# A graph attention and mixture-of-experts kernel: the first loads reordered, W1's load and its casts two batches later

## Chip, cores, metric

One core of one Trainium2 chip. The metric is the device time of one launch in microseconds (us), median of the runs shown. Engines: TensorE (PE, its weight loads PEld), VectorE (DVE), ScalarE (ACT), GpSimd (POOL), SyncE (SP), which here only issues transfers.

## What is computed

For 16 graphs of 512 nodes with 128 features (x, float32) and an int32 adjacency (adj, 16 x 512 x 512), one graph attention layer and one mixture of experts, both with a residual. Cut to what matters:

```python
def _L0_gnn_ref(h, adj, W, a):            # h is the layer norm of x
    Wh = jnp.einsum('bni,oi->bno', h, W)
    a1 = a[0, :OUT_F]
    a2 = a[0, OUT_F:]
    si = Wh @ a1
    sj = Wh @ a2
    e = jax.nn.leaky_relu(si[:, :, None] + sj[:, None, :], negative_slope=ALPHA)
    attention = jnp.where(adj > 0, e, NEG_INF)
    attention = jax.nn.softmax(attention, axis=-1)
    h_prime = jnp.einsum('bij,bjo->bio', attention, Wh)
    return jax.nn.elu(h_prime)
...
x = x + _L0_gnn_ref(_layernorm(x, axis=-1), adj, L0_gnn_W, L0_gnn_a)
x = x + _L0_ffn_ref(_layernorm(x, axis=-1), L0_ffn_Wr, L0_ffn_br, L0_ffn_W1, L0_ffn_b1, L0_ffn_W2, L0_ffn_b2, L0_ffn_gamma, L0_ffn_beta)
```

The second layer (`_L0_ffn_ref`) chooses two of eight experts for each graph by the mean of its normed nodes, applies W1, GELU and W2 of both, mixes them and ends with a layer norm.

## The kernel before

Each engine has a program of its own, written out by hand; semaphores tie them together. Nothing is scheduled by a planner: what stands in an engine's program in a row runs in that row.

**Stages.** B = 16 batches (graphs), each of T = 4 tiles of 128 nodes. The attention stage takes the batches one after another, with several in flight: while VectorE computes the logits of batch n (`logits`), it masks and reduces the destination terms of n+1 (`masked_max`), makes the mask of n+2 (`make_mask`) and the norm's statistics of n+4 (`stats1`). This stage takes about the first 145 us. A short router stage follows, then the experts, batch by batch again.

**One batch of attention.** SP loads x(b) (256 KB), GpSimd loads adj(b) (1 MB of int32, cast to 512 KB of bfloat16 on the way, two buffers). TensorE transposes x (`transpose_x`, L1190 in the profile), ScalarE copies it (`copy_xnt`, L951), TensorE projects it with the prepared weights (`project`, L1199), ScalarE scales the rows by the norm's 1/std into whx (`copy_wh`, L964), which GpSimd made from VectorE's statistics (`norms`, L362 and L367). TensorE spreads the destination terms over the partitions by four transposes into one PSUM bank (`spread_dst`, L1210). VectorE turns adj into a mask of 0 and -2^53 (L498), adds it to the spread terms and takes the row maximum (L505). From the maximum come the shifts (L513 to L525), ScalarE computes the leaky part (L972), VectorE the logits (L534), TensorE transposes them (L1233), ScalarE takes the exponential (L1007), TensorE multiplies with whx (L1248).

**Preparing the weights.** gnn_w, a_src and a_dst (semaphore `s_gw`, 48 when all three are in) are loaded once. VectorE centres gnn_w (L480 to L485), TensorE transposes it and multiplies it with both vectors (L1285 to L1287), ScalarE copies the result to `wh_weights` (L1066, semaphore `s_prep`). No batch can be projected before.

**Order of the first loads.** SP: gnn_w, a_src, a_dst, x(0), x(1); then it waits until adj(0) is in, and issues x(2) and x(3). From x(4) on it waits for the mask of batch b-3. Behind x(5) it issues W1 (1 MB, `w1_parts`), behind x(7) the small weights. GpSimd: the identity matrix and three constants, adj(0), the norm of batch 0, adj(1), the norm of batch 1, adj(2) when mask(0) is made, and so on. VectorE: memsets, the centring, `stats1(0)`, `stats1(1)`, `make_mask(0)`, the four `masked_max(0, t)`.

**W1.** ScalarE casts W1's high part in four pieces (`split_w1_hi`, L1028), one at the end of each of its steps 4 to 7. It is read only after the router.

**Fillers.** `keep_busy` (L1181) issues matmuls on an idle tile whose results nobody reads, in TensorE's waits during the first batches.

Of the kernel before, what the change touches and what calls it, by code (L numbers as in the profile page):

```python
# [22 lines left out]
def gat_moe_kernel(nc, x, adj, gnn_w, gnn_a, w_router, b_router, w1, b1, w2, b2, gamma, beta, out):  # L23
    B, N, D = x.shape
    E, _, F = w1.shape
    T = N // P
# [12 lines left out]
    with ExitStack() as ctx:  # L39
# [10 lines left out]
        x_all = sb("x_all", [P, B, T * D])  # L50
# [205 lines left out]
        def _(sp):  # L256
            def load_x(b):
                if b >= 4:
                    sp.wait_ge(s_x[b % 4], 16 * (b // 4))
                sp.dma_start(x_all[:, b, :].rearrange("p (t d) -> p t d", t=T), x_dram[b]).then_inc(s_x[b % 4], 16)  # L260
# [8 lines left out]

            sp.dma_start(gnn_w_sb[:], gnn_w).then_inc(s_gw, 16)  # L270
            sp.dma_start(a_src[:], gnn_a[0:1, 0:D].rearrange("a d -> d a")).then_inc(s_gw, 16)
            sp.dma_start(a_dst[:], gnn_a[0:1, D:2 * D].rearrange("a d -> d a")).then_inc(s_gw, 16)
            load_x(0)
            load_x(1)
            sp.wait_ge(s_adj[0], 16)
            load_x(2)
            load_x(3)
            for b in range(4, B):
                sp.wait_ge(s_mask, b - 3)
                load_x(b)  # L280
                if b == 5:
                    sp.dma_start(w1_parts[:, :, 1, :].bitcast(F32), w1.rearrange("e p f -> p e f")).then_inc(s_w1raw, 16)
                if b == 7:
                    load_small()
# [43 lines left out]
        def _(pool):  # L328
            nc.gpsimd.memset(ident[:], 0.0).then_inc(s_ident, 1)
# [8 lines left out]
            def load_adj(b):  # L338
                if b >= 2:
                    pool.wait_ge(s_mask, b - 1)  # L340
                nc.gpsimd.dma_start(adj_sb[b % 2][:], adj_dram[b]).then_inc(s_adj[b % 2], 16)
# [60 lines left out]
            load_adj(0)  # L402
# [70 lines left out]
        def _(dve):  # L473
# [4 lines left out]

            dve.wait_ge(s_gw, 48)
# [6 lines left out]

            def stats1(b):
                dve.wait_ge(s_x[b % 4], 16 * (b // 4) + 16)
                if b >= 2:
                    dve.wait_ge(s_norm, 2 * (b - 1))  # L490
                for t in range(0, T, 2):
                    nc.vector.bn_stats(bn12[b % 2][:, 0, t:t + 2, :].rearrange("p t k -> p (t k)"),
                                       x_all[:, b, t * D:(t + 2) * D].rearrange("p (t d) -> p d t", t=2)).then_inc(s_bn1, 1)

            def make_mask(b):

                dve.wait_ge(s_adj[b % 2], 16 * (b // 2) + 16)
                nc.vector.tensor_scalar(mask[:], adj_sb[b % 2][:], 0.0, -MASKED, ALU.is_le, ALU.mult).then_inc(s_mask, 1)  # L498
# [113 lines left out]
            stats1(0)  # L612
# [7 lines left out]
            stats1(2)  # L620
            make_mask(1)
            logits(0, 0)
            masked_max(1, 0)
            logits(0, 1)
# [320 lines left out]
        def _(act):  # L945
# [79 lines left out]
            def split_w1_hi(part):  # L1025
                es = slice(part * E // 4, (part + 1) * E // 4)
                act.wait_ge(s_w1raw, 16)
                nc.scalar.copy(w1_parts[:, es, 0, :], w1_parts[:, es, 1, :].bitcast(F32)).then_inc(s_w1hi, 1)  # L1028
# [53 lines left out]
            for n in range(1, B - 1):  # L1082
                step(n)
                if 4 <= n < 8:
                    split_w1_hi(n - 4)
# [88 lines left out]
        def _(pe):  # L1174
# [28 lines left out]
            def spread_dst(b):  # L1203


                pe.wait_ge(s_wh, T * b + T)
                if b >= 1:
                    pe.wait_ge(s_md, T * b)
                for t in range(T):
                    last = nc.tensor.transpose(dst_ps[:, t * P:(t + 1) * P], whx[b % 3][:, t, 0:1].to_broadcast([P, P]),  # L1210
                                               ident[:])
                last.then_inc(s_dst, 1)
# [66 lines left out]
            keep_busy(8)  # L1279
            pe.wait_ge(s_dconst, 2)  # L1280
            pe.wait_ge(s_const, 1)
            transpose_x(0)
            pe.wait_ge(s_gw, 48)
# [6 lines left out]
            keep_busy(5)  # L1290
# [175 lines left out]
```

## Time and profile before

| what | value |
|---|---|
| median of 3 runs | 279.77 us (279.38 to 282.32) |
| the profiled execution's own time | 279.7 us |
| its span, first to last instruction | 277.9 us |
| busy: PE, DVE, ACT, POOL | 91%, 84%, 81%, 55% |
| HBM read, written | 27.48 MB, 4.20 MB |

The profile is one execution; all times in it are microseconds from the span's start. Busy time is work of the engine itself; waiting on a semaphore, and issuing a DMA, does not count. In the order of events a row gives the start, the duration, the engine, the line of the kernel and the tiles, output to the left of the arrow; in brackets at its end the idle time ahead of it and what ended that. A row with "x4" stands for four instructions in succession. A row of SPq or POOL with DMA_DIRECT2D is only the issue; the transfer runs on the 16 DMA engines, q1 for transfers that SP issued, q0 for GpSimd's.

### The profile page before, as it was taken

Reading aid. Unit: us, or ns where it says so; the run is one execution under the profiler, and the core shown is the slowest. Engines: PE = TensorE matmul, PEld = TensorE weight load, DVE = VectorE, ACT = ScalarE, POOL = GpSimd, SP = SyncE. Lnnn points to the kernel's source line nnn. Section 1 sums busy time; section 2 is a strip of 40 time slices with the busy share of each in tenths; the row PEclk is TensorE's granted clock in tenths of the full one; section 3 lists DMA queues with packets and bytes.
Section 4 is the critical chain, followed back from the end, with each engine's and each line's share of the span. In section 5 each row is a group of like instructions: output and inputs, shape, how many; then the busy total and the mean of one; then the engine's idle time right before and its main releaser. Section 6 shows DMA issues by size and latency. Waiting matters only on the chain. (4 is left out here: it accounts for less than half of the span.)

```text
span 277.9 us, 6310 instructions
## 1 busy us (share of the span) xinstructions
PE 252.9 (91%) x1878; PEld 224.0 (81%) x1878; DVE 232.2 (84%) x658; ACT 224.5 (81%) x513; POOL 152.1 (55%) x228
## 2 busy tenths in 40 slices
PE   7888898999889999999988899999999999999950
PEld 3567897888889898889978448999999999999940
DVE  5599999999999999999999873677777777767556
ACT  3377889999999999999999758778888888877820
POOL 4435288777886779887458312343333444444332
PEclk9999999999999999999999979999999999999996
DMA  6999456654366444550000025576545444543112
GB/s 99 211 221 232 93 99 101 113 101 79 69 99 114 85 80 68 78 75 5 0 4 0 0 96 171 201 249 205 180 162 183 156 167 152 172 154 102 50 39 76
DMA packets 40706, 31.57 MB, mean 114 GB/s; under 512 B 2416, under 2 KB 36624, under 8 KB 40672
## 3 DMA queue, kind: packets, MB, share of 16 engines
q1 hardware_dynamic: 31936, 21.72, 24.5%
q0 software_dynamic: 8736, 9.45, 22.5%
q8 instruction: 15, 0.25, 0.3%
q14 instruction: 19, 0.16, 0.2%
HBM read 27.48 MB, written 4.20 MB: 114 GB/s over the span
## 5 line engine op out<-in xcount | busy, mean ns | idle before, releaser
L1248 PE MATMUL banks<-whx,prob_t 128*128 128x129 f32 x512 | 67.9, 277 | 2.8 <-ACT h_att L982 2.6
L1248 PEld LDWEIGHTS banks<-whx,prob_t 128*128 128x128 f32 x512 | 61.8, 192 | 5.5 <-issue 5.5
L384 POOL TENSOR_SCALAR x_all<-x_all,rstd,nb 128x128 f32<-128x128 f32 x56 | 42.4, 769 | 2.9 <-POOL nb L373 2.7
L1127 ACT ACTIVATE logit<-logit,nb,rstd 128x128 f32<-128x128 f32 x60 | 24.8, 483 | 19.7 <-POOL nb L449 19.7
L1233 PE MATMUL banks<-ident,logit 128*128 128x128 f32 x256 | 36.6, 274 | 4.0 <-DVE logit L534 3.2
L1007 ACT ACTIVATE prob_t<-banks 128x512 f32<-128x512 f32 x64 | 38.2, 641 | 1.8 <-PE banks L1233 1.8
L444 POOL TENSOR_SCALAR veps<-mv 128x4 f32<-128x4 f32 x15 | 6.5, 434 | 55.7 <-DVE mv L841 55.7
L367 POOL TENSOR_TENSOR rstd<-var,minus_half 128x8 f32<-128x8 f32 (+1 forms) x20 | 34.2, 1709 | 0.4
L1233 PEld LDWEIGHTS banks<-ident,logit 128*128 128x128 f32 x256 | 29.0, 141 | 6.3 <-DVE logit L534 5.9
L1402 PEld LDWEIGHTS banks<-w2s,masked_even 128*128 128x128 f32 x256 | 29.8, 192 | 0.6
L1402 PE MATMUL banks<-w2s,masked_even 128*128 128x128 f32 x256 | 29.9, 275 | 0.0
L1387 PE MATMUL banks<-x2t_hi,w_pair 128*128 128x512 f32 x64 | 26.8, 418 | 0.0
L825 DVE TENSOR_TENSOR logit<-banks,x_all 128x512 f32<-128x512 f32 x15 | 10.4, 690 | 19.4 <-PE banks L1402 19.4
L1402 PEld LDWEIGHTS banks<-w2s,leaky 128*128 128x128 f32 x224 | 26.1, 192 | 0.5
L1402 PE MATMUL banks<-w2s,leaky 128*128 128x128 f32 x224 | 26.1, 275 | 0.0
L1389 PE MATMUL banks<-x2t_hi,w_pair 128*128 128x512 f32 x64 | 25.1, 391 | 0.0
L1388 PE MATMUL banks<-x2t_lo,w_pair 128*128 128x512 f32 x64 | 25.0, 390 | 0.0
L362 POOL TENSOR_SCALAR var<-bn 128x8 f32<-128x8 f32 (+1 forms) x20 | 5.7, 283 | 32.6 <-DVE bn L561 20.6
L972 ACT ACTIVATE leaky<-masked_even,shift_neg 128x512 f32<-128x512 f32 x32 | 21.2, 721 | 2.8 <-DVE shift_neg L525 2.8
L534 DVE SCALAR_TENSOR_TENSOR logit<-masked_odd,shift_pos,leaky 128x512 f32<-128x512 f32 x32 | 23.2, 747 | 0.3 <-PE banks L1233 0.2
L972 ACT ACTIVATE leaky<-masked_odd,shift_neg 128x512 f32<-128x512 f32 x32 | 21.3, 720 | 2.5 <-DVE shift_neg L525 2.5
L534 DVE SCALAR_TENSOR_TENSOR logit<-masked_even,shift_pos,leaky 128x512 f32<-128x512 f32 x32 | 23.3, 746 | 0.0
(151 smaller groups left out, 574.0 us busy)
## 6 DMA issues: line engine op xcount, KB each, us to landing
adj_sb<-in_adj_dram POOLq DMA_DIRECT2D x16, 512.0 KB, 7.0
w_pair<-w_parts SPq DMA_DIRECT2D x30, 256.0 KB, 2.3
x_all<-in_x_dram SPq DMA_DIRECT2D x16, 256.0 KB, 3.0
w2r<-in_L_ffn_W_dram SPq DMA_DIRECT2D x32, 128.0 KB, 2.1
out_dram<-prob_t SPq DMA_DIRECT2D x15, 256.0 KB, 2.3
w_parts<-in_L_ffn_W_dram SPq DMA_DIRECT2D x1, 1024.0 KB, 8.1
b_mix<-b_spread POOLq DMA_DIRECT2D x1, 704.0 KB, 5.6
out_dram<-prob_t SPq DMA_DIRECT2D x4, 64.0 KB, 1.6
```

Of the source, the lines that this page charges most:

```text
L367: nc.gpsimd.tensor_tensor(rstd[:, kinds, :], var12[:, kinds, :], minus_half[:].unsqueeze(1).to_broadcast([P, 2, T])[:, kinds, :], ALU.pow) ...
L384: nc.gpsimd.tensor_scalar(x_all[:, b, tile], x1_all[:, b, tile], rstd12[c % 4][:, 1, t:t + 1], nb2[c % 2][:, t:t + 1], ALU.mult, ALU.add). ...
L534: nc.vector.scalar_tensor_tensor(out=logit[:, t, :], in0=masked_dst[b % 2][:, t, :], scalar=shift_pos[b % 2][:, t:t + 1], in1=leaky[:, t, ...
L972: nc.scalar.activation(leaky[:, t, :], masked_dst[b % 2][:, t, :], ACT.Identity, bias=shift_neg[:, t:t + 1], scale=ALPHA).then_inc(s_leaky, 1)
L1007: nc.scalar.activation(prob_t[:, t, :], lt_ps[t % 2], ACT.Exp).then_inc(s_prob, 1)
L1127: nc.scalar.activation(zn[par][:, tile], zs[par][:, tile], ACT.Identity, bias=nb3[par][:, t:t + 1], scale=rstd3[par][:, t:t + 1]).then_inc ...
L1233: last = nc.tensor.transpose(lt_ps[t % 2][:, c * P:(c + 1) * P], logit[:, t, c * P:(c + 1) * P], ident[:])
L1248: last = nc.tensor.matmul(into[:, 0:D + 1], prob_t[:, t, c * P:(c + 1) * P], whx[b % 3][:, c, 2:WHX], start=(c == 0), stop=(c == T - 1))
L1387: nc.tensor.matmul(hid_ps[kc], lo, x2t_hi[par][:], start=True, stop=False)
L1388: nc.tensor.matmul(hid_ps[kc], hi, x2t_lo[par][:], start=False, stop=False)
L1389: nc.tensor.matmul(hid_ps[kc], hi, x2t_hi[par][:], start=False, stop=True).then_inc(s_hid_ps, 1)
L1402: last = nc.tensor.matmul(y_ps[par][:, t * D:(t + 1) * D], hidden[par][:, kc, t * P:(t + 1) * P], w2s[par][:, kc // FC, kc % FC, :], start ...
```

## The change

Seven edits, all in the order of things:
- GpSimd issues adj(0) as its first instruction, ahead of the identity matrix.
- SP issues x(0) ahead of gnn_w, a_src and a_dst.
- x(2) waits for the prepared weights (`s_prep`), no longer for adj(0); x(3) still waits for adj(0).
- W1's load stands behind x(7) instead of x(5), the small weights behind x(9) instead of x(7); ScalarE's four casts of W1 follow steps 6 to 9 instead of 4 to 7.
- VectorE computes the statistics of x(0) ahead of centring the weights; `logits(0, 0)` comes ahead of `make_mask(1)` and `logits(0, 1)` ahead of `masked_max(1, 0)`.
- For batch 0, `spread_dst` waits tile by tile for whx instead of for all four tiles.
- Fewer fillers at the start: 4 instead of 8, a new one behind `transpose_x(0)`, 3 instead of 5 behind `project(0)`.

```diff
+            load_x(0)
             sp.dma_start(gnn_w_sb[:], gnn_w).then_inc(s_gw, 16)
             sp.dma_start(a_src[:], gnn_a[0:1, 0:D].rearrange("a d -> d a")).then_inc(s_gw, 16)
             sp.dma_start(a_dst[:], gnn_a[0:1, D:2 * D].rearrange("a d -> d a")).then_inc(s_gw, 16)
-            load_x(0)
             load_x(1)
+            sp.wait_ge(s_prep, 1)
+            load_x(2)
             sp.wait_ge(s_adj[0], 16)
-            load_x(2)
             load_x(3)
             for b in range(4, B):
                 sp.wait_ge(s_mask, b - 3)
                 load_x(b)
-                if b == 5:
+                if b == 7:
                     sp.dma_start(w1_parts[:, :, 1, :].bitcast(F32), w1.rearrange("e p f -> p e f")).then_inc(s_w1raw, 16)
-                if b == 7:
+                if b == 9:
                     load_small()
...
         def _(pool):
+            nc.gpsimd.dma_start(adj_sb[0][:], adj_dram[0]).then_inc(s_adj[0], 16)
             nc.gpsimd.memset(ident[:], 0.0).then_inc(s_ident, 1)
...
-            load_adj(0)
             norms(0)
             load_adj(1)
...
+            stats1(0)
             dve.wait_ge(s_gw, 48)
             nc.vector.bn_stats(w_stats[:], gnn_w_sb[:]).then_inc(s_centre, 1)
...
-            stats1(0)
             stats1(1)
             make_mask(0)
...
             stats1(2)
+            logits(0, 0)
             make_mask(1)
-            logits(0, 0)
+            logits(0, 1)
             masked_max(1, 0)
-            logits(0, 1)
             masked_max(1, 1)
...
-                if 4 <= n < 8:
-                    split_w1_hi(n - 4)
+                if 6 <= n < 10:
+                    split_w1_hi(n - 6)
...
-                pe.wait_ge(s_wh, T * b + T)
-                if b >= 1:
+                if b >= 1:
+                    pe.wait_ge(s_wh, T * b + T)
                     pe.wait_ge(s_md, T * b)
                 for t in range(T):
+                    if b == 0:
+                        pe.wait_ge(s_wh, t + 1)
...
-            keep_busy(8)
+            keep_busy(4)
             pe.wait_ge(s_dconst, 2)
             pe.wait_ge(s_const, 1)
             transpose_x(0)
+            keep_busy(1)
             pe.wait_ge(s_gw, 48)
...
             project(0)
-            keep_busy(5)
+            keep_busy(3)
             spread_dst(0)
```

SP's row from the program's start, before. The names are the tile written and the tensor read; a mark in brackets names the semaphores waited for, `adj_loaded0` is `s_adj[0]`.

```order
L270 DMA gnn_w_sb<-in_L0_gnn_W_dram 128x128
L271 DMA a_src<-in_L0_gnn_a_dram 128x1
L272 DMA a_dst<-in_L0_gnn_a_dram 128x1
L260 DMA x_all<-in_x_dram 128x4x128 x2
L260 DMA x_all<-in_x_dram 128x4x128 [waits adj_loaded0]
L260 DMA x_all<-in_x_dram 128x4x128
L260 DMA x_all<-in_x_dram 128x4x128 [waits x_loaded0,mask_ready]
L260 DMA x_all<-in_x_dram 128x4x128 [waits x_loaded1,mask_ready]
L282 DMA w1_parts<-in_L0_ffn_W1_dram 128x8x256
```

The same place in the changed program:

```order
L260 DMA x_all<-in_x_dram 128x4x128
L271 DMA gnn_w_sb<-in_L0_gnn_W_dram 128x128
L272 DMA a_src<-in_L0_gnn_a_dram 128x1
L273 DMA a_dst<-in_L0_gnn_a_dram 128x1
L260 DMA x_all<-in_x_dram 128x4x128
L260 DMA x_all<-in_x_dram 128x4x128 [waits gnn_weights_ready]
L260 DMA x_all<-in_x_dram 128x4x128 [waits adj_loaded0]
L260 DMA x_all<-in_x_dram 128x4x128 [waits x_loaded0,mask_ready]
L260 DMA x_all<-in_x_dram 128x4x128 [waits x_loaded1,mask_ready]
L260 DMA x_all<-in_x_dram 128x4x128 [waits x_loaded2,mask_ready]
L260 DMA x_all<-in_x_dram 128x4x128 [waits x_loaded3,mask_ready]
L283 DMA w1_parts<-in_L0_ffn_W1_dram 128x8x256
```

x(0) has moved from the fourth place to the first, x(1) stays the fifth, x(2) has another wait, and W1 stands behind two more loads of x.

VectorE's row from its last memset to the first masked maximum, before (bn12_0 and bn12_1 hold the statistics of batch 0 and 1):

```order
L477 MEMSET whx2 128x524
L480 BN_STATS w_stats<-gnn_w_sb 128x6 [waits gnn_weights_loaded]
L481 TENSOR_SCALAR a_src_scaled<-a_src 128x1
L483 BN_AGGR w_mean<-w_stats 128x2 [waits gnn_weights_centred]
L485 TENSOR_SCALAR gnn_w_centred<-gnn_w_sb,w_mean 128x128 [waits gnn_weights_centred]
L492 BN_STATS bn12_0<-x_all 128x6 [waits x_loaded0]
L492 BN_STATS bn12_0<-x_all 128x6
L492 BN_STATS bn12_1<-x_all 128x6 [waits x_loaded1]
L492 BN_STATS bn12_1<-x_all 128x6
L498 TENSOR_SCALAR mask<-adj_sb0 128x2048 [waits adj_loaded0]
L505 ISA masked_even,dst_max<-mask,banks 128x512 [waits dst_in_psum,mask_ready]
```

The same place in the changed program:

```order
L478 MEMSET whx2 128x524
L485 BN_STATS bn12_0<-x_all 128x6 [waits x_loaded0]
L485 BN_STATS bn12_0<-x_all 128x6
L490 BN_STATS w_stats<-gnn_w_sb 128x6 [waits gnn_weights_loaded]
L491 TENSOR_SCALAR a_src_scaled<-a_src 128x1
L493 BN_AGGR w_mean<-w_stats 128x2 [waits gnn_weights_centred]
L495 TENSOR_SCALAR gnn_w_centred<-gnn_w_sb,w_mean 128x128 [waits gnn_weights_centred]
L485 BN_STATS bn12_1<-x_all 128x6 [waits x_loaded1]
L485 BN_STATS bn12_1<-x_all 128x6
L500 TENSOR_SCALAR mask<-adj_sb0 128x2048 [waits adj_loaded0]
L507 ISA masked_even,dst_max<-mask,banks 128x512 [waits dst_in_psum,mask_ready]
```

The statistics of x(0) have changed places with the centring of the weights; the statistics of x(1), the mask and the maximum keep theirs.

## Rows read from the trace of the kernel before

**Rows 1.** The page's first part: busy us, share of the span, instructions.

```profile
span 277.9 us, 6310 instructions
## 1 busy us (share of the span) xinstructions
PE 252.9 (91%) x1878; PEld 224.0 (81%) x1878; DVE 232.2 (84%) x658; ACT 224.5 (81%) x513; POOL 152.1 (55%) x228
```

**Rows 2.** Busy us (instructions) in stretches; behind them PEclk, DMA share, GB/s.

```profile
12.00:20.00 8.00, 7.29 (x52) 5.10 (x51) 7.90 (x24) 5.63 (x14) 4.21 (x5) 1.00 1.08 227
47.88:56.58 8.70, 8.27 (x71) 7.63 (x70) 8.70 (x26) 8.18 (x21) 6.95 (x10) 1.00 0.53 91
74.02:82.88 8.86, 8.14 (x70) 7.62 (x70) 8.71 (x26) 8.73 (x22) 7.11 (x10) 1.00 0.52 89
```

In a row of this view the five busy times are, in this order, those of PE, PEld, DVE, ACT and POOL.

**Rows 3.** Order of events from 0 to 16 us: start, duration, engine, line, tiles.

```profile
0.74 0.20 POOL L329 MEMSET ident<- 128x128 f32 x1 [0.29 <-POOLq L1454]
0.75 0.39 SPq L270 DMA_DIRECT2D gnn_w_sb<-in_L_gnn_W_dram  x1
...
1.46 3.59 PE L1181 MATMUL banks<-idle_in 128*128 128x512 bf16 x8 [1.46 <-DVE idle_in L474]
...
1.66 0.43 SPq L272 DMA_DIRECT2D a_dst<-in_L_gnn_a_dram  x1
...
1.94 0.99 POOL L341 DMA_DIRECT2D adj_sb<-in_adj_dram  x1 [0.30 <-POOL expert_iota L334]
...
3.73 0.29 DVE L480 BATCH_NORM_STATS2 w_stats<-gnn_w_sb 128x6 f32<-128x128 f32 x1 [0.52 <-DMA a_dst<-in_L_gnn_a_dram]
...
4.28 0.29 DVE L485 TENSOR_SCALAR gnn_w_centred<-gnn_w_sb,w_mean 128x128 f32<-128x128 f32 x1
4.87 0.76 DVE L492 BATCH_NORM_STATS2 bn<-x_all 128x6 f32<-128x256 f32 x2 [0.30 <-DMA x_all<-in_x_dram]
...
5.86 0.42 PE L1285 MATMUL banks<-ident,gnn_w_centred 128*128 128x128 f32 x1
...
6.68 0.27 ACT L1066 COPY wh_weights<-banks 128x130 f32<-128x130 f32 x1
...
7.00 1.16 PE L1199 MATMUL banks<-wh_weights,xnt 128*128 128x130 f32 x8 [0.36 <-ACT wh_weights L1066]
7.03 0.83 POOL L341 DMA_DIRECT2D adj_sb<-in_adj_dram  x1
...
8.00 1.24 PE L1181 MATMUL banks<-idle_in 128*128 128x512 bf16 x5
8.20 1.15 ACT L964 ACTIVATE whx<-banks,rstd 128x130 f32<-128x130 f32 x4 [1.25 <-PE banks L1199]
...
9.40 0.65 PE L1210 MATMUL banks<-ident,whx 128*128 128x128 f32 x4 [0.16 <-ACT whx L964]
10.22 0.77 DVE L492 BATCH_NORM_STATS2 bn<-x_all 128x6 f32<-128x256 f32 x2 [4.59 <-DMA x_all<-in_x_dram]
...
11.61 0.69 DVE L505 CUSTOM_DVE_ANT_0 masked_even<-mask,banks 128x512 f32<-128x512 bf16 x1
```

**Rows 4.** Order of events on SP alone, from 1.5 to 6 us.

```profile
2.13 0.98 SPq L260 DMA_DIRECT2D x_all<-in_x_dram  x2
```

**Rows 5.** Waits from 0 to 34 us: us in total, times, longest; SP's from 0 to 80.

```profile
SPq L260 <- DMA adj_sb<-in_adj_dram: 6.9, 1, 6.9
...
DVE bn L492 <- POOL rstd L367: 0.6, 1, 0.6
```

**Rows 6.** DMA queues: packets, MB, share of 16 engines; two rows 5-6 us, one 8-9.

```profile
q0 software_dynamic: 140, 0.14, 93.8%
q1 hardware_dynamic: 11, 0.01, 2.8%
...
q1 hardware_dynamic: 242, 0.12, 45.3%
```

**Rows 7.** Order of events from 16 to 34 us: W1's load, and the mask of batch 3.

```profile
16.44 0.50 SPq L282 DMA_DIRECT2D w_parts<-in_L_ffn_W_dram  x1
...
30.60 0.68 DVE L498 TENSOR_SCALAR mask<-adj_sb 128x2048 bf16<-128x2048 bf16 x1
```

More of the change, by code:

```diff
@@ L477, in _, with stats1 @@
                 nc.vector.memset(whx[i][:], 1.0).then_inc(s_dconst, 1)
+            def stats1(b):
+                dve.wait_ge(s_x[b % 4], 16 * (b // 4) + 16)
+                if b >= 2:
+                    dve.wait_ge(s_norm, 2 * (b - 1))
+                for t in range(0, T, 2):
+                    nc.vector.bn_stats(bn12[b % 2][:, 0, t:t + 2, :].rearrange("p t k -> p (t k)"),
+                                       x_all[:, b, t * D:(t + 2) * D].rearrange("p (t d) -> p d t", t=2)).then_inc(s_bn1, 1)
+            stats1(0)
             dve.wait_ge(s_gw, 48)
@@ L485, in _ @@
             nc.vector.tensor_scalar(gnn_w_centred[:], gnn_w_sb[:], w_mean[:, 0:1], None, ALU.subtract).then_inc(s_centre, 1)
[L487 to L493, printed above, removed]
             def make_mask(b):
```

## The prediction

> **What bounds the kernel now.** I read the busy shares first, then the stretches, then the order of events of the first 16 us, then the DMA queues. VectorE's share is 84% of 277.9 us [rows 1], an average over stages, so it is read by stage. The table of stretches [rows 2] takes whole batches of the attention stage, one from each mask to the next: VectorE is busy 8.70 of 8.70 us and 8.71 of 8.86. VectorE sets the pace there, and a batch takes about 8.7 us; from the mask at 30.60 [rows 7] to the one at 47.88, where the second stretch begins, it is 17.3 us for two. A chain of batches that runs on one full engine has a simple property: whatever moves its first batch moves everything after it by the same amount. So the first 12 us are worth reading.
>
> There VectorE is nearly idle. Its own rows [rows 3]: the statistics of x(0) at 4.87, then nothing for 4.59 us until x(1) has landed (10.22), the mask, the first masked maximum (11.61). Between x(1) landing and that maximum lie 11.61 - 10.22 = 1.39 us of VectorE work. From 11.61 on the engine hardly stops: 7.90 of the 8 us from 12 to 20 [rows 2]. The maximum needs two inputs: the mask, which needs adj(0) and stands behind the statistics of x(1) in VectorE's queue; and the spread destination terms in PSUM, which TensorE finished at 9.40 + 0.65 = 10.05 [rows 3]. So the load side ends last, by 11.61 - 10.05 = 1.56 us. Both loads of it are late together: SP issued x(0) and x(1) from 2.13 to 3.11 [rows 4] and then waited 6.9 us for adj(0) [rows 5], until 10.0; VectorE's wait for x(1) ended at 10.22. GpSimd had issued adj(0) at 1.94, so it took 8.1 us. x(0) was there by 4.87, 2.7 us after its issue; x(1), issued near 2.6, took about 7.6 us. The queues say why [rows 6]: from 5 to 6 us adj(0)'s queue q0 moved 140 packets and held 93.8% of the engines' time, while q1, with x(1) in it, moved 11; from 8 to 9 us q1 moved 242.
>
> **The change part by part.**
>
> adj(0) first. The DMA leaves GpSimd's queue behind the constants (1.94) for the place of the first memset (0.74): 1.2 us earlier. The identity's memset and select and the two constants behind them, which all lay between 0.74 and 1.94, now end one issue of 0.99 us later, by 2.9 at the latest, ahead of x(0)'s landing; that cover hides them. adj(0) then lands at 10.0 - 1.2 = 8.8.
> GpSimd's issue now lies beside VectorE's first memsets. It did before too: it took 0.99 us there, against 0.83 for the next [rows 3]. By the Trainium skill (SBUF — State Buffer, the box on how DVE blocks software-generated DMA) GpSimd can't write descriptors while VectorE holds the shared port; by that the gain could shrink by the remaining memset, but these rows show at most 0.16 us, which I leave out.
>
> x(0) first. From 2.13 to 0.75, 1.4 us earlier; it lands at about 0.75 + 2.7 = 3.5. VectorE is free from 3.73 - 0.52 = 3.2 on [rows 3], its statistics run 3.5 to 4.25, and what lay between their start (4.87) and the issue of adj(1) (7.03), 2.2 us of statistics and GpSimd's norm, puts that issue at 5.7.
>
> The weights behind it. gnn_w, a_src and a_dst are issued some 0.46 us later each; a_dst at 2.13 in place of 1.66 [rows 3]. Before, VectorE's wait for it ended at 3.73, 2.07 us after its issue. With x(0)'s 256 KB ahead in the same queue I put it at 4.7: the lower bound is 2.13 + 2.07 = 4.2, the upper is that it fares like x(1), which took 7.6 us, so 9.7. I am near the lower bound because adj(0)'s queue starts slowly: x(0), which was under way when q0 began, still took only 2.7 us. From a_dst to the spread terms: VectorE 4.57 - 3.73 = 0.84; TensorE and ScalarE 5.86 to 6.95 = 1.1 for the weights' transposes and copy; the projection 1.16; ScalarE's four copies 1.15, by 0.04 apart; and, since the wait is now by tile, only the last transpose, 0.2 to 0.3. Sum 4.6, with gaps 4.9. So the terms are ready at 4.7 + 4.9 = 9.6, before the mask. TensorE has fewer fillers (4 for 8, 1 new, 3 for 5). The first eight take 3.59 us, 449 ns each, five later ones 1.24 us, 248 ns each [rows 3]: the lower and the higher of its two clock levels (1.2 and 2.4 GHz), although the granted clock prints 1.00. If its gaps delay the rise, this chain has the projections at the lower level and grows by some 1 us; 9.6 becomes 10.6, still near the mask. That costs little.
>
> x(1) itself. Its place in SP's row is the old one, the fifth DMA, issued near 2.6 as before. What gets earlier is the traffic it stands against: adj(0) begins and ends 1.2 us sooner. But adj(1) too comes 1.3 us sooner, and in x(1)'s own queue as many bytes stand ahead. Bounds for its landing: 10.2 - 1.4 = 8.8 if everything slides with x(0), and 10.2 if nothing does; below nothing, 10.2 + 1 if the weights' 256 tiny packets now share turns with q0. I take 9.4, since the later of both loads is held up by adj(0) more than by its own issue. Then the first masked maximum starts at 9.4 + 1.4 = 10.8 in place of 11.61: -0.8 us. The spread terms (9.6) and adj(0) (8.8) are earlier than that.
>
> x(2) is released by the prepared weights (near 7.5) instead of adj(0); its use is the third statistics at about 13.8, no gain, no loss. Logits(0,0) before mask(1) and logits(0,1) before the maximum: the same instructions on a full VectorE, 0. They give TensorE and ScalarE work some 0.6 us earlier, which would matter only if VectorE waited for them. Its one gap there is 0.6 us for GpSimd's rstd [rows 5], which stands behind the statistics of x(3), in the same place as before: 0. Range of this pair: -0.3 to +0.2.
>
> W1's load two batches later (1 MB, issued at 16.44 before [rows 7], near 31 after) clears the stretch 16 to 24 us, where VectorE's only wait is that for rstd [rows 5], and goes beside adj(5), which is issued at about the same time and whose mask is the one at 47.88. Before, the load beside W1 was adj(3), and its mask at 30.60 had no wait [rows 7]. So 0. The four casts of W1 on ScalarE move from steps 4 to 7 to steps 6 to 9. The stretch from 74.02, which holds one, has ScalarE at 8.73 us in place of 8.18 and takes 8.86 us in place of 8.70 [rows 2], so four casts cost at most 0.6 us; moved, I expect the same: 0, with ±0.3.
>
> Sum: -0.8 us. The profiled execution of before took 279.7 us with its span of 277.9, the median of the runs is 279.77, so both bases agree. 279.8 - 0.8 = 279.0 us.
>
> **The rivals.**
>
> A, nothing arrives earlier. x(1) is issued when it was and its queue holds the same bytes; if its landing at 10.2 is its own, VectorE starts as before. For: the same position in SP's row. Against: q1 moves 11 packets in a microsecond while adj(0) has the engines [rows 6], so its landing is not its own. Result 279.7, ±0.3.
>
> B, slower: the weights behind adj(0). q1 nearly stands still when q0 has come into flow, 11 packets against 140 [rows 6]. Before, that met x(1), which had room. Now gnn_w, a_src and a_dst are in it, 384 packets if each of their 3 x 128 rows is one, and the chain of 4.9 us hangs on them. It decides from the point where a_dst lands later than 11.6 - 4.9 = 6.7. At the middle rate between 11 and 242 packets per us, some 100, from 4.4 on they land at 8.2: VectorE's first maximum comes at 13.1, +1.5 us, result 281.3. For: the starved microsecond lies 1.2 us earlier, at 4 to 5 us, where they are. Against: x(0) itself, with q0 beginning, was not held up.
> The Trainium skill (DMA: Bandwidth & Descriptors, "Queues, rings and completion order") says each engine takes turns between queue rows by whole packets of some 9 to 17 descriptors; by that each of the three small loads could wait for a turn of adj(0)'s, which speaks for B. The rows here neither show the turn's length nor deny it.
>
> C, the full slide. x(1) lands at 8.8, a_dst at 4.2, the maximum starts at 10.2 (-1.4), and the earlier logits close part of a gap in the first batches (-0.3): 278.1.
>
> **How the numbers follow.** My forecast (about -0.8) 0.42, A 0.25, C 0.21, B 0.12. The range: down to C with its last gap and the casts' gain (-0.3), 277.7; up to most of B, 280.9. One percent of 279.8 is 2.8 us, about what a measurement of this kernel can tell from no change. Faster than 277.0 would need 1.1 us more than C: 0.04. Slower than 282.6 would need the weights to land at 9.5: 0.03. Within 1%: 0.93.
>
> **What would show it.** In the profile after: GpSimd's adj(0) issue at about 0.75; VectorE's first statistics at 3.5 with x(0) as releaser; centred weights at about 5.1 to 5.6; x(1)'s statistics at 9.4; the first maximum at 10.8; the mask that was at 47.88 at about 47.1, and the first W1 cast two batches (17.4 us) later, less the shift. It is wrong if the first maximum waits for the spread terms (B), if x(1)'s statistics stay at 10.2 (A), or if a shift seen at 11 us is gone by 31 us, which would say that VectorE's queue had slack there.

## The result, and the profile after

The changed kernel takes 285.54 us (median of 4 runs, 282.87 to 287.09) against 279.57 for the kernel before on the same chip: a ratio of 1.0176, 95% interval 1.0114 to 1.0238. Run again later beside the experiments it took 283.98 us (6 runs, 282.89 to 286.77), ratio 1.0121, interval 1.0063 to 1.018. It is slower, and by more than the range allowed. The medians and ranges of this document are over all executions; the ratios leave out four executions that are over 1.5% above their kernel's fastest (two of e2's, one each of e3's and e4's, see below), and are not quotients of the medians.

The order of events of the changed kernel, from 0 to 16 us, as [rows 3] of before:

```profile
0.75 0.45 SPq L260 DMA_DIRECT2D x_all<-in_x_dram  x1
...
1.27 0.99 POOL L330 DMA_DIRECT2D adj_sb<-in_adj_dram  x1 [0.82 <-POOLq L1458]
...
2.27 0.43 SPq L273 DMA_DIRECT2D a_dst<-in_L_gnn_a_dram  x1
...
3.61 0.76 DVE L485 BATCH_NORM_STATS2 bn<-x_all 128x6 f32<-128x256 f32 x2 [0.41 <-DMA x_all<-in_x_dram]
...
7.96 0.29 DVE L490 BATCH_NORM_STATS2 w_stats<-gnn_w_sb 128x6 f32<-128x128 f32 x1 [3.58 <-DMA a_dst<-in_L_gnn_a_dram]
...
8.94 0.45 PE L1289 MATMUL banks<-ident,gnn_w_centred 128*128 128x128 f32 x1 [3.84 <-DVE gnn_w_centred L495]
...
10.38 2.10 PE L1200 MATMUL banks<-wh_weights,xnt 128*128 128x130 f32 x8 [0.36 <-ACT wh_weights L1067]
10.43 0.76 DVE L485 BATCH_NORM_STATS2 bn<-x_all 128x6 f32<-128x256 f32 x2 [1.65 <-DMA x_all<-in_x_dram]
11.11 0.68 DVE L500 TENSOR_SCALAR mask<-adj_sb 128x2048 bf16<-128x2048 bf16 x1
...
12.28 1.48 PE L1182 MATMUL banks<-idle_in 128*128 128x512 bf16 x3
12.52 1.15 ACT L965 ACTIVATE whx<-banks,rstd 128x130 f32<-128x130 f32 x4 [2.19 <-PE banks L1200]
...
13.56 1.06 PE L1213 MATMUL banks<-ident,whx 128*128 128x128 f32 x4
...
14.78 0.69 DVE L507 CUSTOM_DVE_ANT_0 masked_even<-mask,banks 128x512 f32<-128x512 bf16 x1 [2.99 <-PE banks L1213]
```

Read the brackets. VectorE's mask was there at 11.11 + 0.68 = 11.79, the first masked maximum begins at 14.78, 2.99 us of idleness later, and what ended the idleness is no load any more but TensorE's spread (L1213). Follow that back: whx at 12.52 waited for the projection, the projection (10.38) for the prepared weights, they for the centred gnn_w, and that for a_dst, which VectorE awaited for 3.58 us, until 7.96. a_dst was issued at 2.27. So the chain behind the weights, which had 1.56 us of room before, now ends last. The clock has a share in this: the projection takes 2.10 us where it took 1.16 [rows 3]. Busy time by stretch, as [rows 2]; the third number from the right is the granted clock:

```profile
8.00:15.00 7.00, 5.71 (x23) 4.83 (x24) 2.33 (x8) 1.42 (x5) 2.29 (x3) 0.52 0.95 207
51.67:60.36 8.69, 8.25 (x71) 7.62 (x70) 8.69 (x24) 8.16 (x21) 6.94 (x10) 1.00 0.59 108
158.00:164.00 6.00, 4.45 (x29) 2.73 (x27) 4.68 (x18) 4.02 (x11) 1.47 (x4) 1.00 0.00 0
164.00:176.00 12.00, 10.64 (x36) 6.38 (x37) 6.50 (x27) 5.83 (x12) 1.72 (x2) 0.72 0.35 122
167.28:179.28 12.00, 11.90 (x45) 8.49 (x46) 4.40 (x17) 8.35 (x18) 2.24 (x4) 0.72 0.47 150
```

From 8 to 15 us TensorE had the lower of its two levels (1.2 GHz) almost throughout, after it had been busy for only 1.10 of the 4 us from 4 to 8. At the start this printed number can't be relied on alone: in the second profile of this kernel (e12) and in e1, e2, e5, e7 and e8 it is 1.00 from 0 to 15 us, though the projection takes 2.10 us there as well. So the level at the start is read from the durations below, 2.10 or 1.16 us for the projection. In the middle (second row) nothing has changed: VectorE is full, the batch takes 8.69 us. From 164 to 176 us the clock is low again for part of the stretch, and most of that row sits in the first experts; the last row is their first 12 us. The same three stretches in the kernel before, whose experts begin at 163.36:

```profile
158.00:164.00 6.00, 5.23 (x22) 2.29 (x22) 4.60 (x20) 1.96 (x7) 1.09 (x1) 0.72 0.04 13
164.00:176.00 12.00, 12.00 (x70) 9.70 (x69) 6.21 (x19) 9.74 (x18) 1.74 (x3) 1.00 0.60 199
163.36:175.36 12.00, 12.00 (x71) 9.66 (x70) 5.91 (x19) 9.32 (x19) 2.13 (x4) 1.00 0.58 192
```

There the low clock fell into the router, where TensorE has mostly fillers to run; here it falls into the experts, where TensorE is the bound. In the first 12 us of the experts it issued 71 matmuls before, 45 after.

Where the time went, by marks that both traces have:

| mark | before | after | added since the mark above |
|---|---|---|---|
| first masked maximum, batch 0 | 11.61 | 14.78 | +3.17 |
| mask of batch 3 | 30.60 | 34.38 | +0.61 |
| mask of batch 15 | 134.23 | 138.22 | +0.21 |
| first matmul of the experts (L1387, L1391) | 163.36 | 167.28 | -0.07 |
| last row of VectorE | 275.56 | 282.59 | +3.11 |

The sum is 7.03, the spans differ by 285.0 - 277.9 = 7.1 us. Four terms to explain: 3.2 at the start, 0.6 in the first batches, 0.2 in the steady part, 3.1 in the experts.

### The profile page after: what moved, and what is told of

It is laid out like the page before. It is cut to its first block and busy times, and to the rows that moved or that the text cites. A ratio compares the mean times of both kernels' runs of the same rounds, so it can differ in the third digit from the quotient of the medians.

```text
span 285.0 us, 6299 instructions
## 1 busy us (share of the span) xinstructions
PE 254.8 (89%) x1871; PEld 227.0 (80%) x1873; DVE 232.5 (82%) x658; ACT 224.5 (79%) x513; POOL 152.2 (53%) x228
## 5 line engine op out<-in xcount | busy, mean ns | idle before, releaser
L1391 PE MATMUL banks<-x2t_hi,w_pair 128*128 128x512 f32 x64 | 27.9, 436 | 0.4 <-ACT w_pair L1111 0.4
L1392 PE MATMUL banks<-x2t_lo,w_pair 128*128 128x512 f32 x64 | 25.9, 404 | 0.0
L1393 PE MATMUL banks<-x2t_hi,w_pair 128*128 128x512 f32 x64 | 25.7, 402 | 0.0
L1138 ACT ACTIVATE masked_even<-banks,b_sel 128x512 f32<-128x512 f32 x32 | 19.8, 676 | 5.0 <-PE banks L1393 5.0
L507 DVE CUSTOM_DVE_ANT_0 masked_even<-mask,banks 128x512 f32<-128x512 bf16 x32 | 21.2, 670 | 3.0 <-PE banks L1213 3.0
```

The source lines that it names most:

```text
L1391: nc.tensor.matmul(hid_ps[kc], lo, x2t_hi[par][:], start=True, stop=False)
L1392: nc.tensor.matmul(hid_ps[kc], hi, x2t_lo[par][:], start=False, stop=False)
L1393: nc.tensor.matmul(hid_ps[kc], hi, x2t_hi[par][:], start=False, stop=True).then_inc(s_hid_ps, 1)
```

## Experiments

**The start: which load stands in whose way.** Theory Q came out of the rows above: the small loads lie behind x(0) in SP's queue and fall under adj(0)'s traffic. Rival K says that the low clock, through the fewer fillers, makes the start late. The first four kernels ran together; the kernel before took 280.08 us beside them.

e1, SP's and VectorE's old order, adj(0) still first:

```diff
-            load_x(0)
             sp.dma_start(gnn_w_sb[:], gnn_w).then_inc(s_gw, 16)
...
+            load_x(0)
             load_x(1)
...
-            stats1(0)
             dve.wait_ge(s_gw, 48)
...
+            stats1(0)
             stats1(1)
```

> The changed kernel with SP's old order (gnn_w, a_src, a_dst, x(0), x(1)) and VectorE's old order (centring ahead of the statistics of x(0)); adj(0) stays GpSimd's first instruction. Theory Q (the three small loads stand in SP's queue behind x(0) and fall under adj(0)'s traffic, a_dst lands at 7.9 us): the wait for a_dst ends by 4.0 us, the first masked maximum starts at 10.5 to 11.3 in place of 14.78, the time is that of the kernel before or up to 1 us under it, 278.5 to 280. Rival K (TensorE's granted clock, low from 8.2 to 15.1 us because of the fewer fillers, is what makes the start late): the weights come early but the projection and the spread still run at the low clock, the maximum starts after 12.5, and the time stays above 281.

Measured: 286.46 us (4 runs, 284.52 to 287.78), ratio 1.0213 (1.0154 to 1.0272). The weights did come early and the time did not. The order of events of this kernel:

```profile
3.81 0.29 DVE L489 BATCH_NORM_STATS2 w_stats<-gnn_w_sb 128x6 f32<-128x128 f32 x1 [0.60 <-DMA a_dst<-in_L_gnn_a_dram]
...
8.77 1.47 DVE L485 BATCH_NORM_STATS2 bn<-x_all 128x6 f32<-128x256 f32 x4 [4.13 <-DMA x_all<-in_x_dram]
```

a_dst is in at 3.8, as in the kernel before, and now it is x(0) that comes at 8.77. The time is in the range of rival K, but not by K's way: the projection is slow here too (2.10 us), and yet what comes first is a load. And Q as I had put it is too narrow: a large load in the small ones' place is held up as well. Either of them delays everything, since in TensorE's program the transposes of x(0) stand ahead of the weights' and both ahead of the projection. In this kernel the weights were centred by 4.65 us and yet waited for x(0); the first maximum came at 16.01, 1.2 us later than in the changed kernel. The queues of this kernel from 4 to 5 us, then from 5 to 6:

```profile
q0 software_dynamic: 156, 0.16, 115.5%
...
q0 software_dynamic: 130, 0.13, 92.7%
q1 hardware_dynamic: 48, 0.02, 16.0%
```

From 4 to 5 us q1 has no row at all: not one packet of x(0), issued at 2.13. In the changed kernel the small loads fare differently. Its queues from 4 to 5 us:

```profile
DMA packets 155, 0.10 MB, mean 102 GB/s; under 512 B 56, under 2 KB 155, under 8 KB 155
...
q0 software_dynamic: 99, 0.10, 77.6%
q1 hardware_dynamic: 56, 0.00, 5.4%
```

All 56 packets of q1 are small ones. They go on, 65 of them from 5 to 6 us and 74 of q1's 105 from 6 to 7, but slowly: with adj(0) 0.67 us later (e2, below) 272 small packets pass from 3 to 4 us.

e8, adj(0) first as the only edit to the kernel before (run later, beside e5 to e7):

```diff
+            nc.gpsimd.dma_start(adj_sb[0][:], adj_dram[0]).then_inc(s_adj[0], 16)
             nc.gpsimd.memset(ident[:], 0.0).then_inc(s_ident, 1)
...
-            load_adj(0)
             norms(0)
```

> The kernel before with one part of the change: adj(0) as GpSimd's first instruction. Theory Q (adj(0)'s traffic, once in flow, holds back whatever SP's queue has not begun to move, here x(0)): x(0) lands at 8 to 9 us in place of 4.84, the first masked maximum starts at 13 or later in place of 11.61, time 281.5 to 284. Rival (it took the whole change to lose time): adj(0) lands 0.6 us earlier and nothing is lost, 279 to 280.

Measured: 286.03 us (4 runs, 283.84 to 287.52), ratio 1.0204 (1.012 to 1.0289); the landing and the maximum are as expected, the time is 2 us above the range.

```profile
8.78 1.47 DVE L492 BATCH_NORM_STATS2 bn<-x_all 128x6 f32<-128x256 f32 x4 [4.13 <-DMA x_all<-in_x_dram]
...
16.44 0.69 DVE L505 CUSTOM_DVE_ANT_0 masked_even<-mask,banks 128x512 f32<-128x512 bf16 x1 [5.60 <-PE banks L1210]
```

x(0) at 8.78 and the first maximum at 16.44, 4.8 us late. At the first maximum this one line of the change costs, alone, more than the whole change (3.2); by the times of the runs the two can't be told apart. Within the change, putting x(0) ahead of the weights repairs part of the harm: x(0) gets through, and a_dst is held up in its stead.

e2, the opposite: everything but that line.

```diff
-            nc.gpsimd.dma_start(adj_sb[0][:], adj_dram[0]).then_inc(s_adj[0], 16)
...
+            load_adj(0)
             norms(0)
```

> The changed kernel with adj(0) issued where it was, behind GpSimd's constants (about 1.9 us), and x(0) still ahead of the weights. Theory Q in its strong form (it takes both, x(0) ahead and adj(0) early): the weights slip through before adj(0)'s traffic flows, a_dst lands by 5.5, the maximum starts below 12.5, time 279.5 to 281.5. Rival Q2 (x(0) ahead is enough; the small packets are slow whoever is beside them): a_dst lands at 7 or later, the maximum starts above 14, time above 282.5.

Measured: 279.94 us (10 runs), ratio 1.0002 (0.9963 to 1.0041). The strong form of Q holds:

```profile
DMA packets 381, 0.07 MB, mean 67 GB/s; under 512 B 272, under 2 KB 381, under 8 KB 381
...
q1 hardware_dynamic: 362, 0.05, 27.9%
q0 software_dynamic: 19, 0.02, 27.1%
```

These are its queues from 3 to 4 us: the small loads are nearly through when adj(0)'s packets begin. Its order of events:

```profile
4.84 0.29 DVE L490 BATCH_NORM_STATS2 w_stats<-gnn_w_sb 128x6 f32<-128x128 f32 x1 [0.53 <-DMA a_dst<-in_L_gnn_a_dram]
...
7.28 2.10 PE L1200 MATMUL banks<-wh_weights,xnt 128*128 128x130 f32 x8 [0.36 <-ACT wh_weights L1067]
8.89 0.76 DVE L485 BATCH_NORM_STATS2 bn<-x_all 128x6 f32<-128x256 f32 x2 [3.22 <-DMA x_all<-in_x_dram]
...
11.32 0.69 DVE L507 CUSTOM_DVE_ANT_0 masked_even<-mask,banks 128x512 f32<-128x512 bf16 x1 [1.08 <-PE banks L1213]
```

adj(0) issued at 1.94 in place of 1.27, 0.67 us, decides whether a_dst lands at 4.8 or at 7.5 to 8.0 (7.96, 7.46 and 7.85 in the changed kernel, e12 and e7, which start alike). x(1) comes at 8.89, the mask is ready by 9.57 + 0.68 = 10.25, and still VectorE waits 1.08 us for TensorE, whose projection again takes 2.10 us.

**The clock at the start.** e3 is the changed kernel with the old fillers:

```diff
-            keep_busy(4)
+            keep_busy(8)
...
             transpose_x(0)
-            keep_busy(1)
...
-            keep_busy(3)
+            keep_busy(5)
```

> The changed kernel with the old fillers on TensorE (8, none behind the transposes of x(0), 5). Theory Q: a_dst lands at 7.9 as before, the maximum still starts above 13, at most 1.6 us earlier than 14.78, from projection and spread at the high clock; time 282 to 286. Rival K: granted clock high from 6 us on, start as in the kernel before, time below 281.

Measured: 282.75 us (4 runs, 282.66 to 287.58), ratio 1.0103 (1.0075 to 1.0131). The first maximum comes at 14.01, 0.77 us earlier than in the changed kernel; a_dst was in at 7.78 in place of 7.96, so about 0.6 us are the fillers': from a_dst to the first maximum it takes 6.23 us here and 6.82 or 6.83 in the changed kernel, e7 and e12. The start stays 2.4 us late. Q carries the most of it, K a part. The projection took 2.10 us in this profile too: TensorE stood still for 2.84 us waiting for the weights, and fillers ahead of a wait don't help in it.

e5 is e2 with these old fillers.

> The changed kernel with adj(0) at its old place and the old fillers (8, none, 5). Theory Q plus K (with the loads in time, what holds the spread terms up is the low granted clock of the start: in the run with adj(0) late it was low until 10.66 us and the projection took 2.10 us in place of 1.16): clock high from about 6 us, projection about 1.2 us, first masked maximum at 10.1 to 10.5, mask of batch 3 at 29.3 to 29.8, time 278.3 to 279.2, 0.5 to 1.4 us under the kernel before. Rival: the start isn't carried to the end, mask of batch 3 again at 30.6, time 279.5 to 280.5.

Measured: 279.69 us (12 runs, 278.95 to 282.14), ratio 0.9983 (0.9944 to 1.0021). The forecast of theory Q plus K missed: in the profiled execution the clock was low all the same, the projection took 2.10 us (7.12 to 9.22) and the maximum started at 11.63. So the old fillers don't secure the higher level. Over all profiles, the five with the fewer fillers (after, e1, e2, e7, e12) have the slow projection; of the nine with the old ones six have the fast one (before, e4, e6, e9, e10, e11), and e3, e5 and e8 have not.

```profile
10.87 0.60 PE L1213 MATMUL banks<-ident,whx 128*128 128x128 f32 x4
...
11.63 0.69 DVE L507 CUSTOM_DVE_ANT_0 masked_even<-mask,banks 128x512 f32<-128x512 bf16 x1 [1.13 <-PE banks L1213]
```

The next kernel's profile had the clock high.

**The order of the logits.** e6 is e5 with the old order:

```diff
-            logits(0, 0)
             make_mask(1)
-            logits(0, 1)
+            logits(0, 0)
             masked_max(1, 0)
+            logits(0, 1)
```

> The same with the old order of logits(0,0), mask(1), logits(0,1) and the first masked maximum of batch 1 as well. Theory R (the new order costs about 0.3 us on VectorE: with adj(0) late the first maximum came 0.3 us earlier than in the kernel before and the mask of batch 2 at the same time): the mask of batch 3 comes 0.2 to 0.4 us earlier than without this edit. Rival: the order is free, the masks of both runs agree within 0.1 us.

Measured: 278.9 us (12 runs, 278.64 to 281.86), ratio 0.996 (0.992 to 1.0).

```profile
6.56 1.16 PE L1200 MATMUL banks<-wh_weights,xnt 128*128 128x130 f32 x8 [0.36 <-ACT wh_weights L1067]
...
8.64 0.65 PE L1213 MATMUL banks<-ident,whx 128*128 128x128 f32 x4
...
10.40 0.69 DVE L507 CUSTOM_DVE_ANT_0 masked_even<-mask,banks 128x512 f32<-128x512 bf16 x1
...
29.39 0.68 DVE L500 TENSOR_SCALAR mask<-adj_sb 128x2048 bf16<-128x2048 bf16 x1
```

Here the projection takes 1.16 us and the maximum follows the mask without a wait, at 10.40. Up to there e5 and e6 are the same program with a_dst in at 4.55 and 4.58, so the two profiles price the low clock: the spread ends at 9.29 instead of 11.47, 2.2 us, of which 1.2 reach the first maximum.

The masks of batch 3 can't be compared as the expectation has it, since the clocks of the two profiles differ. The stretch from the first maximum to that mask can: 29.39 - 10.40 = 18.99 us, and in e5 30.94 - 11.63 = 19.31. The kernels with the old order have 18.98 to 19.00 (before, e4, e6, e8, e9, e10, e11), e2, e3 and e5 with the new one 19.31. The new order costs 0.32 us. The changed kernel has 19.60, e12 19.75, e1 and e7 19.43: 0.1 to 0.4 us come on top. In these four profiles the spread of batch 0 took 1.06 us, so the clock was still low just ahead of the first maximum; that this is the cause is not shown, and e8, with the same slow spread and the old order, has 19.00. The rows of e2 show where the new order costs:

```profile
15.34 0.75 DVE L536 SCALAR_TENSOR_TENSOR logit<-masked_even,shift_pos,leaky 128x512 f32<-128x512 f32 x1 [0.23 <-ACT leaky L973]
16.01 0.69 DVE L500 TENSOR_SCALAR mask<-adj_sb 128x2048 bf16<-128x2048 bf16 x1
```

VectorE is full there, and logits(0,0), moved ahead of the mask, waits 0.23 us for ScalarE's leaky part; before, the mask filled that time.

**W1's load and casts.** e4 is the kernel before with these alone:

```diff
-                if b == 5:
+                if b == 7:
                     sp.dma_start(w1_parts[:, :, 1, :].bitcast(F32), w1.rearrange("e p f -> p e f")).then_inc(s_w1raw, 16)
-                if b == 7:
+                if b == 9:
                     load_small()
...
-                if 4 <= n < 8:
-                    split_w1_hi(n - 4)
+                if 6 <= n < 10:
+                    split_w1_hi(n - 6)
```

> The kernel before with one part of the change: W1's load and the small loads two batches later, ScalarE's casts in steps 6 to 9. Theory: nothing waits for these loads, so 279.6, within 0.5 us. Rival W (W1 beside adj(4) and adj(5), or the casts in later, fuller batches, cost something): 280.2 or more, and the mask of batch 15 comes over 0.5 us later than 134.23.

Measured: 280.17 us (10 runs, 279.48 to 284.04), ratio 1.0012 (0.997 to 1.0053); the mask of batch 15 at 134.16. Rival W is out as it was put. By the stretch from the mask of batch 3 to that of batch 15 something small is left: 134.16 - 30.31 = 103.85 us, and 103.84 in the changed kernel, against 103.63 before and in e8. That is 0.2 us, below what the times resolve, but all profiles agree: 103.57 to 103.63 in the four kernels with W1 at its old place (before, e8, e10, e11), 103.74 to 103.85 in the ten with it late. Whether the load or the casts cost it was not tested.

**The clock in the experts.** e4 gave an unplanned control. Its profiled execution took 282.67 us, 2.9 over that of before, with the mask of batch 15 at the same place; all of it came behind:

```profile
164.00:176.00 12.00, 11.90 (x51) 8.88 (x51) 4.01 (x14) 8.71 (x16) 1.74 (x3) 0.72 0.49 157
```

From the experts' first matmul to the last row of VectorE: 278.53 - 163.22 = 115.31 us. Before it is 275.56 - 163.36 = 112.20, in the changed kernel 282.59 - 167.28 = 115.31. The same 3.1 us appear without the change at the start. So the start isn't needed for them; it is where the clock falls. Low stretches of that kind lie in the router in the profiles of before, e3, e5, e6 and e8, in the first experts in after, e1, e4 and e12, and in neither in the other five. e7 asked whether TensorE's gaps in the router call it down, with the changed kernel and one edit:

```diff
-        WARM = (11, 3, 2, 7)
+        WARM = (11, 3, 4, 10)
```

> The changed kernel with more fillers on TensorE in the router stage (4 for 2 and 10 for 7). Theory C (of the 7 us lost in the profiled execution about 3 come from the granted clock at its lower level from 168.67 to 175.50 us, in the first experts, after TensorE's gaps in the router): the clock holds, or falls earlier and in fewer executions; median 283 to 284, and few runs over 285. Rival: the clock falls whatever stands in these gaps, median 285 to 287, as for the changed kernel itself.

Measured: 283.54 us (6 runs, 282.9 to 284.27), ratio 1.0112 (1.006 to 1.0163). No execution was over 284.3. The unedited kernel, ten runs in two groups, had six up to 284.32 and four from 286.42 to 287.09. If the fillers did nothing, six low ones in e7 would still come in one case of nine. e7 in its profile:

```profile
158.00:164.00 6.00, 4.87 (x32) 3.05 (x31) 4.69 (x17) 3.73 (x11) 1.20 (x3) 1.00 0.00 0
164.00:176.00 12.00, 11.31 (x57) 7.60 (x56) 6.90 (x28) 8.62 (x18) 2.83 (x4) 1.00 0.36 120
```

The second group of the unedited kernel is e12.

> The changed kernel again, unedited, beside the others on one chip, to see how its executions fall. Theory C: steps as in the other kernels, the lowest near 282.9, others near 284.3 and 286.8, so most of the distance between its median and 283 is the clock in the experts; the start is late in each (first maximum 14 to 15 us). Rival: the start itself varies, and a profile in a fast execution shows the first maximum under 12.5.

Its profiled execution is one of the long ones: first maximum at 14.29, mask of batch 15 at 137.88, experts' first matmul at 166.93, last row at 282.25, again 115.3 us. The start is late in this execution as in the first; no profile of a short execution of the unedited kernel exists, but e7's is one in all but the fillers (maximum at 14.67, mask of batch 15 at 137.94, and 112.34 us of experts).

The same fillers in the kernel before, e10:

> The kernel before with the router fillers alone. Theory C: the start of the kernel before (mask of batch 3 at 30.6) and no executions over 281; median 279.4 to 279.8. Rival: the same scatter as the kernel before, up to 283.

Measured: 279.9 us (12 runs, 279.32 to 280.74), ratio 0.9978 (0.9952 to 1.0004), where the kernel before ran from 279.17 to 283.23 beside it, six of 29 over 282. None of the twelve was, which by chance alone happens in one case of ten. The median hardly moves. Taken together, the three kernels with these fillers (e7, e10, and e9 below) have none of 30 executions in their upper step, the same kernels without them 11 of 51 (four of ten, six of 29, and one of e6's twelve, at 281.86). Chance would do that in under one case of 100, an estimate from these counts. So the fillers very likely take the upper step away. They aren't the only way to miss it: e11, without them, has none in ten.

**What of the change is worth keeping.** e11 is the kernel before with x(0) ahead of the weights and its statistics ahead of the centring, nothing else:

```diff
+            load_x(0)
             sp.dma_start(gnn_w_sb[:], gnn_w).then_inc(s_gw, 16)
...
-            load_x(0)
             load_x(1)
...
+            stats1(0)
             dve.wait_ge(s_gw, 48)
...
-            stats1(0)
             stats1(1)
```

> The kernel before with one part of the change: x(0) ahead of the weights on SP and its statistics ahead of the centring on VectorE. Theory Q: adj(0)'s traffic starts at about 4 us, behind x(0) and two of the small loads, so a_dst lands by 5 and x(1) and adj(0) about 1 us earlier than before, first maximum at 10.2 to 10.6 when the clock rises early, mask of batch 3 at 29.2 to 29.7, lowest executions near 278.7. Rival (the gain of the run with adj(0) late came from another part, the wait of x(2) or the spread by tile): first maximum at 11.3 or later, lowest executions at 279.3.

Measured: 278.71 us (10 runs, 278.35 to 280.46), ratio 0.9948 (0.9914 to 0.9982): faster than the kernel before by 0.5%.

```profile
4.42 0.29 DVE L489 BATCH_NORM_STATS2 w_stats<-gnn_w_sb 128x6 f32<-128x128 f32 x1 [0.22 <-DMA a_dst<-in_L_gnn_a_dram]
8.95 0.76 DVE L484 BATCH_NORM_STATS2 bn<-x_all 128x6 f32<-128x256 f32 x2 [3.69 <-DMA x_all<-in_x_dram]
...
10.34 0.69 DVE L506 CUSTOM_DVE_ANT_0 masked_even<-mask,banks 128x512 f32<-128x512 bf16 x1
```

x(1) is there at 8.95 in place of 10.22, though SP issues it no earlier, and the shift of 1.27 us at the first maximum is still 1.33 at the mask of batch 15 (132.90 against 134.23). Part of this is scatter: e4 and e10, which start like the kernel before, have the first maximum at 11.32 and 11.29, so the gain there is 0.95 to 1.27 us. e6 and e9, which have the other wait of x(2) and the spread by tile as well, start their first maximum at 10.40 and 10.38, so the rival of the expectation falls and these two parts bought nothing. The lowest executions differ by 0.82 (278.35 against 279.17). Last, e9, e6 with the router fillers:

> The changed kernel with adj(0) late, old fillers at the start, old logit order (278.9 us), and the router fillers (4 for 2, 10 for 7). Theory C (the upper steps of the scatter, near 280.1 and 281.9 beside 278.8, are executions in which the clock fell in the router or the first experts): all executions within 278.3 to 279.3, median 278.7, under the kernel before with an interval clear of 1. Rival: the scatter stays, some executions over 281.

Measured: 278.86 us (12 runs, 278.7 to 279.98), ratio 0.9936 (0.9903 to 0.9968). Ten of the twelve lie between 278.70 and 278.96, two near 279.9; the expectation allowed none there, so the fillers do not take away the step a microsecond up. e9 and e11 beat both kernels, and the runs don't tell them apart.

## Why the prediction was wrong

The frame held, the likeliest case did not. That the attention stage passes on whatever its first batch loses is what the marks show: 3.78 us late at the mask of batch 3, the changed kernel is 3.99 us late at that of batch 15.

**The weights behind x(0).** The step that failed is "I put it at 4.7". It measured 7.96. Its own upper bound, 9.7, and rival B, 8.2 and a first maximum decided by the spread terms, had it; B got 0.12. I had leaned on x(0), which in the kernel before was nearly through when adj(0)'s traffic began: by 4.5 us q0 had moved 14 packets, and in the half microsecond behind it q1 moved two, so x(0) was through. That says nothing of a transfer with most of its packets still to come. In the changed kernel 121 of the some 320 small packets had passed by 4.0 us, in e2 295 had; the rest of them went at 56 to 74 a microsecond beside adj(0), below even the 100 of rival B. That they had begun did not spare them. e2 and e11 are what 4.7 describes (4.84 and 4.42), with adj(0) late. The forecast moved both loads forward and took the landing of a_dst from a picture in which only x(0) had moved.

**adj(0) first.** "1.2 us earlier" measured 0.67: GpSimd began the issue at 1.27, after 0.82 us of idleness behind its sequencer, not at 0.74. It took 8.6 us to land (8.1 before, 7.7 in e4 and e10), so 9.9 in place of 10.0, where 8.8 was forecast. e8 and e1 give the sign of this edit that I had wrong: alone it costs 4.8 us at the first maximum. I had asked what hides the moved memsets and not what the moved DMA starves. That was the question that x(1)'s 7.6 us in [rows 3] posed.

**x(1).** Forecast 9.4, measured 10.43 (9.79 in e12), within its own bounds, which reach 11.2 where the small packets share turns. In e11 it is 8.95, so the part of the reasoning that x(1)'s landing is set by the traffic about it was right, and rival A's "its landing is its own" is refuted.

**The clock.** "That costs little" was sized too small and placed wrong. From the weights to the first maximum I had put 4.9 us and "some 1 us" more at the lower level; it took 14.78 - 7.96 = 6.8, 1.9 more. With the clock high, in e6, the spread ends 4.7 us after the weights (4.58 to 9.29), as forecast. The microsecond is the projection's (2.10 for 1.16). The rest is mostly in what follows: the three fillers behind the projection take 1.48 us at this level and stand ahead of the spread, which begins at 13.56, when they end, though ScalarE's first whx is ready near 12.8 (an estimate: 12.52 and a quarter of 1.15); and the spread itself takes 1.06 us for 0.65. So the wait tile by tile, of which I took only the last transpose, bought nothing. As the chain behind the weights now ended last, all of it came on top, and B's price of 1.5 us was low for that reason.

**Logits.** "The same instructions on a full VectorE, 0": measured 0.32 us, outside the 0.2 allowed. A full engine is where the order isn't free: an instruction moved ahead of one that was ready waits in its place.

**W1.** 0 ± 0.3; measured 0.2. Right.

**The experts.** No term of the sum, no rival. Of the 7.1 us in the profiled executions 3.1 are here. It is a step that the kernel before has as well, in six of 29 executions beside e9 to e12 and 15 of all its 74, against four of ten for the changed one. Whether the change makes it likelier these counts don't settle. Without it the change costs 3.6 to 4.0 us (by the mask of batch 15 in e12 and in the first profile), and that is 283 to 284, still outside the range.

The Trainium skill's rule of turns between queue rows (DMA: Bandwidth & Descriptors, "Queues, rings and completion order") spoke for B, and B came. In the changed kernel the traces agree: q1's small packets pass beside q0's all the way, 56 beside 99 from 4 to 5 us. So they do from 6 to 7 us in the kernel before, 92 beside 133. They don't agree for a load of x that is next in the queue: from 4 to 5 us in e1 q1 has no packet, and taking turns does not give that. These traces don't show what holds the packets up in that microsecond.

## What to carry to other kernels

Ask of a transfer that is moved forward whom it will hold up, and take the answer from a transfer in the trace that had as many of its packets still to come. Put ahead of a heavy GpSimd load whatever a long chain hangs on, and check that its packets are through before the load's flow; 0.67 us decided here. Count the fillers that stand ahead of a critical instruction at the lower clock level too. And before a few microseconds are put down to an edit, compare the clock of the bound stage in both profiles, or fill the gaps that call it down in both kernels.

## What the runs showed that I had not expected

- A transfer that SP issues shortly before GpSimd's cast load of adj starts to flow stays away for some 2 us beyond its usual start: x(0), issued at 2.13 in e1 and e8, has no packet from 4 to 5 us and is in at 8.8, against 4.9 when adj(0) comes 0.67 us later.
- The first instruction of GpSimd's program, if it is a DMA, begins at 1.27 (after, e1, e3, e7, e8, e12); a memset in its place began at 0.74.
- The granted clock's low stretch costs about 0.1 us in the router (from the mask of batch 15 to the experts 29.13 us before, 29.06 in e9) and 3.1 us in the first experts: from the experts' first matmul to the end it is 112.2 to 112.3 us in ten profiles and 115.3 in the four others (after, e1, e4, e12).
- x(0) ahead of three small loads made adj(0) land sooner too, with adj(0)'s own issue untouched at 1.94: it took 6.6 us in e11 where it takes 8.1 in the kernel before, and 7.7 in e4 and e10, which start alike.
